# Attention's maximum pass on 32-row strips of the tensor engine, with new buffers and a new written order

## What is computed

```python
q = rope((x @ W_q) by head); k = rope((lat @ W_uk) by head)      # layer 0; layer 1 has small per-head weights, no rope
scores = einsum('bhqd,bhkd->bhqk', q, k) / sqrt(8)
scores = where(causal, scores, -inf)
attn = softmax(scores, axis=-1)
out = einsum('bhqk,bhkd->bhqd', attn, v)
```

## Time and profile before

| what | us |
|---|---|
| three runs | 1503.78, 1506.66, 1509.22 (median 1506.66) |
| profiled execution, first to last instruction | 1517.5 |
| attention, layer 0, first maximum matmul to last output | 109.8 to about 602.5 |
| attention, layer 1 | 815.8 to about 1306 |
| PE / DVE / ACT busy over the whole span | 1211.4 / 951.7 / 683.7 |

### The profile page before, as it was taken

One profiled execution on the slowest core, in us unless ns is written; L12 is line 12 of the kernel. 1 busy time (PEld: TensorE's weight loads), 2 busy tenths in 40 slices (PEclk: granted clock), 3 DMA queues, 4 the chain that ended last, 5 costly groups with the idle time before them and its releaser, 6 DMA issues. The chain is left out here.

```text
span 1517.5 us, 20983 instructions
## 1 busy us (share of the span) xinstructions
PE 1211.4 (80%) x7346; PEld 524.4 (35%) x7347; DVE 951.7 (63%) x2598; ACT 683.7 (45%) x895; POOL 187.9 (12%) x257
## 2 busy tenths in 40 slices
PE   2917999999799998319553899999989999676984
PEld 2502333333233343207421223233333334444663
DVE  6627888888678772301163788888868775342443
ACT  1302465665566666103230445566656667421331
POOL 4110000000000000344410000000000000054442
PEclk9857999999899999559875899999999999777997
DMA  4154000230502000022216310140120000011113
GB/s 128 31 118 68 16 16 15 39 74 16 67 15 73 3 3 1 22 63 57 76 50 123 52 43 19 35 87 25 26 44 2 3 3 2 1 35 43 47 47 104
DMA packets 41740, 64.10 MB, mean 42 GB/s; under 512 B 5440, under 2 KB 27872, under 8 KB 41328
## 3 DMA queue, kind: packets, MB, share of 16 engines
q1 hardware_dynamic: 37328, 53.95, 16.4%
q0 software_dynamic: 4320, 8.92, 1.7%
HBM read 45.55 MB, written 18.92 MB: 42 GB/s over the span
## 5 line engine op out<-in xcount | busy, mean ns | idle before, releaser
L792 ACT ACTIVATE probs_at<-st 128x1024 f32<-128x1024 f32 (+3 forms) x640 | 545.7, 897 | 382.4 <-PE st L747 236.4
L810 DVE TENSOR_REDUCE mxp_at<-mx 128x1 f32<-128x512 f32 x768 | 498.4, 685 | 96.0 <-PE mx L716 95.1
L716 PE MATMUL mx<-ks,qs 128*128 128x512 bf16 (+3 forms) x1280 | 379.9, 368 | 84.9 <-DVEq L801 33.2
L747 PE MATMUL st<-qs,ks 128*128 128x512 bf16 (+3 forms) x1280 | 355.6, 354 | 13.9 <-DMA qs<-shrow_at 12.6
L812 DVE CUSTOM_DVE_ANT_0 junk_at<-mx,maskN 128x384 f32<-128x384 f32 (+3 forms) x512 | 241.2, 485 | 104.7 <-PE mx L716 102.4
L763 PE MATMUL av<-probs_at,vs 128*32 128x512 f32 (+3 forms) x2560 | 301.7, 543 | 0.2
L716 PEld LDWEIGHTS mx<-ks,qs 128*128 128x128 bf16 x1280 | 104.8, 98 | 437.7 <-DVE mxp_at L810 183.6
L747 PEld LDWEIGHTS st<-qs,ks 128*128 128x128 bf16 x1280 | 123.4, 99 | 111.0 <-ACT probs_at L792 21.8
L1027 POOL DMA_INDIRECT perm<-rows,pos x64 | 63.3, 989 | 512.6 <-SPq L1136 248.4
L750 PE MATMUL st<-maskTb,identb 128*128 128x128 bf16 x512 | 100.9, 222 | 0.0
L763 PEld LDWEIGHTS av<-probs_at,vs 128*32 128x32 f32 x2560 | 50.6, 108 | 107.2 <-issue 96.7
(11 more groups left out here) (232 smaller groups left out, 1027.8 us busy)
## 6 DMA issues: line engine op xcount, KB each, us to landing
qs<-q_parts SPq DMA_DIRECT2D x63, 128.0 KB
ks<-k_parts SPq DMA_DIRECT2D x18, 384.0 KB
w_sb<-in_w_dram SPq DMA_DIRECT2D x16, 256.0 KB, 3.1
q_parts<-part_pj SPq DMA_DIRECT2D x12, 256.0 KB, 3.0
k_parts<-part_pj SPq DMA_DIRECT2D x12, 256.0 KB, 4.7
perm<-in_pad_dram SPq DMA_DIRECT2D x1, 2600.0 KB, 11.6
rows_f<-perm SPq DMA_DIRECT2D x39, 65.0 KB, 1.8
ks<-k_parts SPq DMA_DIRECT2D x12, 192.0 KB
```

The source lines that it names most:

```text
L716: pe.matmul(buf[:, 0:w], QS[p][:, j, (4 * Q + qb) * P:(4 * Q + qb + 1) * P], KS[p][:, j, c * CH:c * CH + w], start=True, stop=True).then_i ...
L747: mm = pe.matmul(st[half][:, y, off:CH], KS[p][:, j, kb * P:(kb + 1) * P], QS[p][:, j, Q * CH + off:(Q + 1) * CH], start=True, stop=True, ...
L792: act.activation(probs[:, s % 2, 2 * half:2 * half + 2, off:CH], st[half][:, :, off:CH], ACT.Exp, scale=SCALE).then_inc(exp_done[half], 1)
L810: ins = v.tensor_reduce(dst, buf[:, 0:w], AX.X, ALU.max)
```

## The change

- **Layout.** Each head's rows are placed by head. Head j has its four main products (high and middle parts of q times high and middle parts of k, 4 x 8 = 32 rows) on partitions 32j to 32j+31, its other five products (40 rows) and its two shift rows at `AUX[j]` elsewhere. QS is zero and KS one where nothing is loaded. A matmul of the scores still takes all 128 rows.
- **Maximum matmul.** It takes the 32-row strip alone (`tile_position=(32*j, 0)`), so the maximum comes from four products in place of nine. Head j is now the innermost loop of a unit's maxima, so successive ones are on different strips.
- **Buffers.** MXBUF 3 to 4, each with a semaphore of its own. `st` is three banks of one head each in place of two of two heads; `probs` is three steps deep; the buffers of shifts and maxima go from 4 to 2.
- **ACT.** It takes the exponent of one head at a time (4 a step, 128x512 at most) and makes the copies of "turn" and "attT" that DVE made.
- **Transfers.** A group's loads are 12 + 16 DMAs in place of 10 + 3, with the same number of rows; a turn's shift is 4 DMAs of 2 rows in place of one. The ones and zeros from DRAM are gone; POOL sets all of QS and KS.
- **Order.** `schedule()` is new, and writes ACT's order as well; UNITS is group by group.

```diff
-SHIFT0 = 96
-MXBUF = 3
+RT = P // GH
+AUX = (RT, 2 * RT, 0, 0)
+SHIFT = [a + 5 * HD for a in AUX]
+MXBUF = 4
+STBUF = 3
+PB = 3
-UNITS = [(0, 0), (0, 1), (0, 2), (1, 1), (0, 3), (1, 2), (1, 3), (1, 0),
-         (2, 2), (2, 3), (3, 3), (2, 1), (3, 1), (2, 0), (3, 0), (3, 2)]
+UNITS = [(0, Q) for Q in (0, 1, 2, 3)] + [(1, Q) for Q in (1, 2, 3, 0)] + [(2, Q) for Q in (1, 2, 3, 0)] + [(3, Q) for Q in (3, 2, 1, 0)]
...
 def schedule():
+    maxes = [(u, (g, Q, j, qb, c)) for u, (g, Q) in enumerate(UNITS) for qb in range(TPC) for c in range(Q + 1) for j in range(GH)]
+    lat, rate = .15, 2370.
+    rows = [0.] * GH
...
+        all_rows = max(rows)
+        found = []
+        if chores:
+            t, kind, x = min(chores)
+            found.append((max(pe, t, all_rows, free[b] + lat) - .2, "chore"))
+        if s < NST and ready[UNIT[s]] is not None and s < a + PB:
+            found.append((max(pe, ready[UNIT[s]] if STEPS[s][2] == 0 else 0., st_free[n % STBUF] + lat, all_rows) - .1, "scores"))
+        if a < NST and probs_ready[a] is not None:
+            found.append((max(pe, probs_ready[a] + lat, all_rows, av_free + lat if STEPS[a][2] == 0 else 0.), "values"))
+        if k < len(maxes) and loaded[maxes[k][1][0]] is not None:
+            found.append((max(pe, rows[maxes[k][1][2]], free[b] + lat, loaded[maxes[k][1][0]]) - .05, "max"))
+        t, what = min(found)
+        if what == "max":
+            pe = max(t + .05, pe) + .03
+            rows[x[2]] = pe + w / rate
+            dve = max(dve, rows[x[2]] + lat) + .08 + w * .00104
...
+        elif what == "scores":
+            pe = max(t + .1, pe) + (CH - off) / rate + (.08 if on_diagonal(s) else .01)
+            rows = [pe] * GH
+            act = max(act, pe + lat) + .05 + (CH - off) * .000833
...
+        elif what == "values":
+            pe = max(t, pe) + 4 * (CH - step_off(a)) / rate + .05
+            rows = [pe] * GH
+            if a in LAST[:NG - 2]:
+                loaded[LAST.index(a) + 2] = pe + 12.
...
+            if kind in ("turn", "attT"):
+                act = max(act, pe + lat) + .48
+                if kind == "turn":
+                    ready[x] = act + 2.4
```

```diff
 def load_q(sp, m, L, dram, g, cols, done):
+    for j in range(GH):
+        sp.dma_start(to(RT * j, RT), src(0, [[0, 2], [T, 2 * HD]])).then_inc(done, 16)
+        sp.dma_start(to(AUX[j], 3 * HD), src(2, [[0, 3], [T, HD]])).then_inc(done, 16)
+        sp.dma_start(to(AUX[j] + 3 * HD, 2 * HD), src(0, [[T, 2 * HD]])).then_inc(done, 16)
 def load_k(sp, m, L, dram, g, cols, done):
+    for j in range(GH):
+        sp.dma_start(to(RT * j, 2 * HD), src(0, [[0, 2], [T, HD]])).then_inc(done, 16)
+        sp.dma_start(to(RT * j + 2 * HD, 2 * HD), src(1, [[0, 2], [T, HD]])).then_inc(done, 16)
+        sp.dma_start(to(AUX[j], 2 * HD), src(0, [[T, 2 * HD]])).then_inc(done, 16)
+        sp.dma_start(to(AUX[j] + 2 * HD, 3 * HD), src(2, [[0, 3], [T, HD]])).then_inc(done, 16)
...
-                        sp.dma_start(QS[g % 2][SHIFT0:SHIFT0 + 2 * GH, :, Q * CH:(Q + 1) * CH],
-                                     shrow[:, u % 4, :].unsqueeze(1).to_broadcast([2 * GH, GH, CH])).then_inc(shift_set[u % 4], 16)
+                        for j in range(GH):
+                            sp.dma_start(QS[g % 2][SHIFT[j]:SHIFT[j] + 2, j, Q * CH:(Q + 1) * CH],
+                                         shrow[2 * j:2 * j + 2, n % 2, :]).then_inc(shift_set[n % 2], 16)
...
-                        pe.matmul(buf[:, 0:w], QS[p][:, j, (4 * Q + qb) * P:(4 * Q + qb + 1) * P],
-                                  KS[p][:, j, c * CH:c * CH + w], start=True, stop=True).then_inc(mx_ready, 1)
+                        pe.matmul(buf[:, 0:w], QS[p][strip, j, (TPC * Q + qb) * P:(TPC * Q + qb + 1) * P],
+                                  KS[p][strip, j, c * CH:c * CH + w], start=True, stop=True, tile_position=(RT * j, 0)).then_inc(mx_ready, 1)
...
+                def exponent(s, j):
+                    off, e = step_off(s), EB + s * GH + j
+                    if j == 0 and SB + s >= PB:
+                        act.wait_ge(av_done, SB + s - PB + 1)
+                    act.wait_ge(st_ready, e + 1)
+                    act.activation(probs[:, s % PB, j, off:CH], st[e % STBUF][:, off:CH], ACT.Exp, scale=SCALE).then_inc(exp_done, 1)
```

More of the change, by code:

```diff
@@ L89, in schedule @@
[L89 to L95 removed]
+    maxes = [(u, (g, Q, j, qb, c)) for u, (g, Q) in enumerate(UNITS) for qb in range(TPC) for c in range(Q + 1) for j in range(GH)]
+    last_max = [max(k for k, (x, _) in enumerate(maxes) if x == u) for u in range(NU)]
+    lat, rate = .15, 2370.
+    pe = dve = act = 0.
+    rows = [0.] * GH
+    free = [0.] * MXBUF
@@ L162 @@
+    return pe_order, act_order, rot, (pe, act, dve)
+PE_ORDER, ACT_ORDER, ROT, _ = schedule()
 NROT = len(ROT)
-ATTT_AT = {x: k for k, (kind, x) in enumerate(ROT) if kind == "attT"}
-NORM_AT = {x: k for k, (kind, x) in enumerate(ROT) if kind == "norm"}
+AT = {x: k for k, x in enumerate(ROT)}
+USES = [len(range(b, NROT, MXBUF)) for b in range(MXBUF)]
+TURN_NO = {x: n for n, x in enumerate(x for kind, x in ROT if kind == "turn")}
+OF_UNIT = [[k for k, (kind, x) in enumerate(ROT) if kind == "max" and x[:2] == UNITS[u]] for u in range(NU)]
@@ L728, in rotate @@
                         mm.then_inc(mx_ready, 1)
-                    elif kind == "out":
-                        pe.wait_ge(mx_free, RB + ATTT_AT[x] + 1 + MXBUF)
+                    else:
+                        pe.wait_ge(*released(AT["attT", x]))
                         for qb in range(TPC):
@@ L783, in evacuate @@
                     if u >= 2:
[L784 removed]
+                        act.wait_ge(mx_ready, RB + AT["norm", u - 2] + 1)
                     act.copy(avs[:, u % 2, :], avb[:]).then_inc(av_free, 1)
[L787 to L795 removed]
@@ L796, in _, with turned @@
-                evacuate(NU - 1)
+                def turned(k):
+                    kind, x = ROT[k]
+                    buf, free = mxb[k % MXBUF], mx_free[k % MXBUF]
+                    act.wait_ge(mx_ready, RB + k + 1)
+                    if kind == "attT":
+                        act.copy(attT[:], buf[:]).then_inc(free, 1)
+                    else:
+                        n = TURN_NO[x]
+                        if UB + n >= 2:
+                            act.wait_ge(shift_set[n % 2], 16 * GH * (L * NU // 2 + n // 2))
+                        act.copy(shrow[:, n % 2, :], buf[:].bitcast(BF)[0:2 * GH, 0:CH]).then_inc(shift_row, 1)
+                        act.wait_ge(shift_row, UB + n + 1)
+                        act.sem_inc(free, 1)
@@ L798, in _ @@
+                for item in ACT_ORDER:
+                    if item[0] == "exp":
+                        exponent(item[1], item[2])
+                    elif item[0] == "evacuate":
+                        evacuate(item[1])
+                    else:
+                        turned(item[1])
             @block.vector
             def _(v):
-                if L == 0:
-                    v.sem_inc(mx_free, MXBUF)
                 for k, (kind, x) in enumerate(ROT):
-                    buf = mxb[k % MXBUF]
+                    if kind in ("turn", "attT"):
+                        continue
+                    buf, free = mxb[k % MXBUF], mx_free[k % MXBUF]
@@ L1517, in layout @@
     ang = (np.arange(T, dtype=np.float32)[None, :] * inv[:, None]).astype(np.float32)
-    ones = np.zeros((GH, 2 * GH, T), np.dtype("bfloat16"))
-    for j in range(GH):
-        ones[j, 2 * j:2 * j + 2] = 1
     dw = np.zeros((E8 + 1, 3 * P, D), np.float32)
```

349 lines of the change are left out of this document (146 added, 203 removed).

## The result

| kernel | us, median of 4 | ratio to before | profiled span, us | granted clock |
|---|---|---|---|---|
| before | 1507.94 (1503.78 to 1513.86) | 1 | 1517.5 | 0.889 |
| changed | 1670.52 (1669.7 to 1671.37) | 1.106 [1.102, 1.110] | 1668.1 | 0.820 |

The changed kernel is 10.6% slower. The direction was forecast, the size was not: 1670.5 lies beyond the end of the range at 1605. Cut into stretches, the two profiled spans show where the time went (each row ends where the next begins).

A forecast was written before the change was run, and what follows sets the result against it. PE was taken to bound attention's mixed stretches, DVE next. Terms -11 - 11 - 13 + 40 + 8 + 8 = +21 us, added to the median of 1506.66, gave 1528 us, 1.4% slower; range 1445 to 1605.

The forecast's parts named there:

- What bounds the kernel: Attention's mixed stretches: PE is the bound at 2.77 us a full step, DVE next at some 2.4.
- Part 1: Maximum matmuls on 32-row strips: overlap saves 0.43 us a step, added shape changes take back 0.36; -11 us in all.
- a granted clock below 0.9 over attention, which I have not priced: Listed sign that the forecast is wrong: PE's clock over attention under 0.9; no size given.
- Part 2: ACT's exponents by head fit under PE; deeper score and `probs` buffers take away half of 22.3 us of waits: -11 us.
- Part 3: Group loads: with units group by group, group 3's keys land in time and PE's 12.6 us of waits go: -13 us.
- Part 4: Turns behind the loads of groups 2 and 3: four waits of some 10 us on PE, +40 us.
- Part 5: SP's issues: 28 DMAs a group at 0.34 us, 9.5 us against 4.6, +8; four issues a turn, another +8.
- Part 6: POOL's clearing of QS and KS ends by 46, before its next work at 59.38: no cost; 14 us without that cover.
- A: Rival on full steps: cheap row switch or maxima in fours, DVE decides; 1472 us, 1432 without blocked turns; chance 0.22.
- B: Rival on turns: shifts go out before the loads and are not held; 1488 us; chance 0.18.
- C: Rival on maxima: they go one by one or in smaller groups; 1616 us with three groups a step; chance 0.12.
- D: Rival on strips: they do not overlap, three maxima take 0.65 us, the step 3.17; 1611 us; chance 0.06.

The follow-up runs named there:

- x9: x6 with the maximum matmul on all 128 rows instead of strips, exponent's scale a hundredth; 1531.8 us, 1.011 of the kernel before.
- x11: x6 with strips in units 0 to 3 and the maximum on all 128 rows in units 4 to 15; 1562.4 us, 1.019 of the kernel before.
- x6: x5, and group 1's loads also go out behind the turn of unit 1 in place of unit 0; 1558.0 us, 1.027 of the kernel before.
- x5: The changed kernel with the loads of groups 2 and 3 held until the next turn's shift is issued; 1574.0 us, 1.038 of the kernel before.
- d1: The kernel before with the new order of units and nothing else; 1566.5 us, 1.033 of the kernel before.
- e1: The changed kernel with ACT in place of SP issuing the turn's shift transfers; 1642.1 us, 1.072 of the kernel before.
- x7: x6 with an extra 128-row matmul ahead of each maximum matmul of units 1 to 3; 1632.0 us, 1.076 of the kernel before.
- x8: x6 with a planner that reckons 0.12 us for each change of shape; 1567.2 us, 1.034 of the kernel before.

## Why the prediction was wrong in size

**What bounds the kernel: right.** PE at 2.77 us a step decides the mixed stretches, and DVE is next.

**Part 1 (strips, -11): overlap and price right, sum wrong.** Overlap is near full (starts 3 to 4 ns apart), a change costs about 0.10 where 0.12 was taken, and the step shown takes 2.77. Of 52 full steps with four maxima, 28 have the order traced and take 2.77 us (median), no less than the 2.78 of before. Another 22 take all four maxima at once and last 2.40. The same two kinds of step take 2.72 in x9, without strips. (The 2.62 and the 2.83 or 2.89 in the expectations of x9 and x11 come from a grouping that mixes widths.) In the stretches at the full clock the strips save 5.7 us a layer, 11.4 together. That this is the forecast's 11 is luck: it was to come from 192 steps of the order traced, and came from groups of four. Over all of attention the strips cost 25 us (x6 against x9) in place of saving 11. The term that failed is the one that the prediction named and left out, "a granted clock below 0.9 over attention, which I have not priced". The changed kernel had 0.85, x6 0.89 and 0.88, and x9 0.95 and 0.94 (layers 0 and 1).

Beside it, "TensorE: Matmul & The Clock Gate", Part 3, of the Trainium skill gives 3.07x for four 32-row matmuls. Starts 3 to 4 ns apart agree with overlap of that order. What the kernel gains by it does not follow from that figure.

**Part 2 (ACT, -11): wrong, by a misread row.** The 22.3 us in the earlier trace rows are the sum over PE and its weight loads. The view by lines of the kernel before keeps them apart:

```profile
L747 PE MATMUL st<-qs,ks 128*128 128x512 bf16 (+3 forms) x1280 | 355.6, 354 | 13.9 <-DMA qs<-shrow_at 12.6 <-ACT probs_at L792 0.5
L747 PEld LDWEIGHTS st<-qs,ks 128*128 128x128 bf16 x1280 | 123.4, 99 | 111.0 <-ACT probs_at L792 21.8 <-DMA qs<-shrow_at 13.9 <-issue 7.7
```

The matmuls themselves had waited 0.5 us of the 22.3. There was nearly nothing to take away. After, the weight loads wait 256.8 us for ACT in 520 waits, and the matmuls 2.6: here a weight load that waited cost its matmul next to nothing.

**Part 3 (`ks`, -13): right.** No wait for `ks` is left.

**Part 4 (turns behind loads, +40): the step that failed.** Place, count and cause are as forecast: four waits, at units 5 and 9 of both layers. Each was to be 10 us and is 22.5; x5 prices them at about 100 us in all. The number was taken from a shift that lands with the load 31 us after its issue, with 20 us of steps ahead of it. d1 shows that this holds for large loads: 29 to 32 us, 19 us of work, 12 us each. In the changed kernel SP needed 0.82 us an issue, so the 28 issues that part 5 put at 9.5 us took 23, the shift went out 18 us behind the turn, and PE went on 37 to 39 us behind the load's first issue. It had also run out of work after 15 to 16 us. The first issues of a load, 0.4 to 0.7 us, are already twice what was taken; some later ones run to 2.07.

The same holds for group 1's load, where part 4 took nothing: PE's wait at the turn of unit 1, 5.7 and 4.0 us before, became 12.6 and 11.8. x6 takes 16 us back there. This is the second omission: the trace of before already showed this wait, and a load that is issued more slowly had to lengthen it.

**Part 5 (issues, +16): low.** The first maximum matmul came 10.3 us later in layer 0 and 1.4 in layer 1, where 5 and 3 were reckoned; of the 10.3, 6 are part 6's. A wait of 2.8 us for the shift of unit 0 in layer 1 became 10.5, one of 3.2 is new in layer 0, and ten more waits of 1.0 to 1.7 make 14 us.

**Part 6 (POOL at nothing): wrong by about 6 us.** POOL's own next work covers the clearing as said: its four sets of QS and KS end at 38, its next work comes at 64.8. But that next work is late itself, 64.8 in place of 59.4, and what is late is DVE, in the layer norm while POOL clears. The timelines of DVE, first before:

```profile
22.56 2.21 DVE L304 TENSOR_SCALAR a_ln<-mv_ln 128x4 f32<-128x4 f32 x1
28.57 3.96 DVE L322 TENSOR_SCALAR xn_pj<-x,mv_ln,y_ln 128x128 f32<-128x128 f32 x4
```

then after:

```profile
22.07 5.54 DVE L318 TENSOR_SCALAR a_ln<-mv_ln 128x4 f32<-128x4 f32 x1
31.31 7.29 DVE L336 TENSOR_SCALAR xn_pj<-x,mv_ln,y_ln 128x128 f32<-128x128 f32 x4
```

The last of POOL's four clearings:

```profile
31.00 6.94 POOL L583 MEMSET ks<- 128x8192 bf16 x1
```

The same instructions of DVE take 0.17 and 1.1 us once POOL is done, and the long ones end with POOL's clearings: the 5.54 us end at 27.6, as the second clearing does, and the first of the four that start at 31.31 ends at 38.0, as the last clearing does. PE's first matmul behind them comes at 38.7 in place of 32.6, and SP's first store of `q_parts` at 73.3 in place of 67.4. All kernels here that start from the changed one show POOL's next work at 64.4 to 65.5, all that start from before at 58.0 to 59.4. No run takes the clearing away alone.

Against the forecast's +21, the profiled span grew by 151. Part 4 is 50 to 60 of the difference (by its waits, 90 - 40, or by x5, 100 - 40), the strips 36 (25 + 11), unit 1's turns 15, part 2 11, POOL's clearing 6, and the rest of part 5 some 15. That makes 133 to 143 of 130 (151 - 21), with terms that overlap and come from different runs; no closer account is claimed.

**The rivals.** A came in part: its maxima in fours are there in 22 of the 52 steps, and such a step takes 2.40 us. But 28 take 2.77, and what A was to save went to the clock. B (turns not held) is excluded by the four waits, C (single maxima) by groups of three and four, D (no overlap) by the starts. None of them held the case that came: the forecast's own mechanism at more than twice its size, and a granted clock of 0.85.

## What to carry to other kernels

A small transfer that an engine waits for must not stand behind a large load on an in-order queue: look up, for each load that is moved, which small transfer comes next on that queue, and send the load behind it (here that is worth 7 to 8% of the kernel's time). When a load is cut into more transfers, price the issues at their own durations, since nearly equal bytes in 28 pieces took SP five times as long as in 12. A shorter step is worth little if the granted clock falls with it: compare clocks over the same stretch before counting columns, and don't add up the waits of weight loads with those of matmuls. And that an engine's own next work is far off does not make its work free: see what the other engines do meanwhile.

## What the runs showed of the hardware that was not expected

- **Issues.** 12 large loads held SP for 4.3 us (0.34 each for q). The 28 of the changed kernel held it for 23 us, 0.4 to 0.75 each for the most part and up to 2.07. Which limit sets this is open. Over 318 to 338 us the 16 DMA engines were by far not full:

```profile
318.00:338.00 20.00, 0.77 (x8) 0.08 (x8) 1.35 (x4) 0.28 (x1) 0.00 (x0) 0.57 0.25 82
```

A DMA share of 0.25 and 82 GB/s, while an 8 KB shift needed 15 us from issue to use. What held it was most likely its place behind other transfers on SP's queue: issued by ACT in e1, 311.0 to 313.4, it had landed by 323.97, before SP had issued the last of the load. A queue of its own on an idle engine was not tried.
- **Strips.** Matmuls on four 32-row strips start 3 to 4 ns apart, four take 0.327 us to the next scores matmul where one takes 0.317, and a change between 32 and 128 rows costs 0.10 us.
- **POOL and DVE.** While POOL cleared QS and KS, DVE instructions that take 0.17 us later took 2.2 to 5.5 us and ended with one of POOL's clearings.
- **Clock.** With the same list of work PE got 0.57 in the first 50 us when the maxima took 32 rows, 0.75 when they took 128 (x6, x9); with 128-row matmuls added it was busy 45.7 of 50 us and got 0.50 (x7). Strips in another order got 0.68 (x8). Which property of the work the grant follows stays open.
